# Moving the stack transfers of q to SyncE's queue and the loads of x one block later, in a fused attention and channel-mix kernel

## What is computed

```python
# attention: 16 heads of 16, in 4 groups that share k and v; token i sees tokens i-127 to i
q = (x @ Wq + bq); k = x @ Wk + bk; v = x @ Wv + bv
scores = einsum(q, k) / sqrt(16)
scores = where(mask, -1e9, scores)
out = softmax(scores) @ v
x = layernorm(x + (out @ Wo + bo))
# channel mix
xr = mu_r * x + (1 - mu_r) * x_prev
xk = mu_k * x + (1 - mu_k) * x_prev
x = layernorm(x + sigmoid(xr @ W_r.T) * (square(relu(xk @ W_k.T)) @ W_v.T))
```

## Time and profile before

| what | value |
|---|---|
| median of 3 runs | 511.7 us (510.95 to 513.18) |
| profiled execution | 514.49 us |
| its span, first to last instruction | 512.8 us |
| TensorE busy | 413.8 us, 81% |
| weight loads | 253.1 us, 49% |
| DVE busy | 340.2 us, 66% |
| ScalarE busy | 272.8 us, 53% |
| GpSimd busy | 290.0 us, 57% |
| DMA moved | 39.24 MB, 77 GB/s on average |
| mean granted TensorE clock | 0.902 |

### The profile page before, as it was taken

The page is one execution under the profiler, slowest core; times in us unless marked ns, Lnnn a source line. Parts: engine busy times, 40 slices in busy tenths (PEclk is TensorE's granted clock), DMA queues, the critical chain, the costliest instruction groups (busy, mean ns, idle before and its releaser), DMA issues.

```text
span 512.8 us, 8346 instructions
## 1 busy us (share of the span) xinstructions
PE 413.8 (81%) x2494; PEld 253.1 (49%) x2494; DVE 340.2 (66%) x851; ACT 272.8 (53%) x566; POOL 290.0 (57%) x466
## 2 busy tenths in 40 slices
PE   5407767998699959998699958998699949999963
PEld 2105344565356545565356545565355635666452
DVE  5315534588577848788497848688578838888543
ACT  3301334665447735775367735775467725787642
POOL 5500334565557736675477736675567737777721
PEclk9856567999889978999799999999899969999988
DMA  7770493035802384034902384045902390000000
GB/s 287 140 90 7 112 150 59 7 82 92 155 11 66 75 136 91 12 83 94 168 13 64 76 131 98 11 87 94 164 13 66 74 133 13 13 12 24 22 10 31
DMA packets 49356, 39.24 MB, mean 77 GB/s; under 512 B 32160, under 2 KB 40864, under 8 KB 49184
## 3 DMA queue, kind: packets, MB, share of 16 engines
q1 hardware_dynamic: 42256, 25.73, 21.7%
q10 hardware_dynamic: 7056, 12.98, 16.7%
HBM read 26.38 MB, written 12.06 MB: 75 GB/s over the span
## 4 chain that ended last, share of the span: by engine, by line
PE 45%; DVE 19%; DMA 19%; ACT 5%; issue 5%; SPq 4%; POOL 1%; ACTq 1%; DVEq 0%; POOLq 0%
DMA qs<-max_rows 11%; PE av_ps L963 8%; PE proj_ps L876 8%; PE score_ps L949 7%; DMA qs<-q_parts 6%; PE gen L1054 5%; DVE neg_max L688 5%; PE max_ps L932 4%; PE gen L1043 4%; SPq L321 3%; PE gen L997 3%; DVE mix L763 3%; DVE q_tiles L680 2%; DVE y L782 2%; PE gen L1032 2%
## 5 line engine op out<-in xcount | busy, mean ns | idle before, releaser
L386 POOL TENSOR_SCALAR_AFFINE_SELECT probs<-probs 128x512 f32<-128x512 f32 x252 | 167.5, 674 | 156.4 <-ACT probs L521 154.0
L521 ACT ACTIVATE probs<-score_ps 128x512 f32<-128x512 f32 x252 | 148.5, 598 | 139.8 <-PE score_ps L949 118.3
L949 PE MATMUL score_ps<-qs,ks 98*128 98x512 bf16 x252 | 102.4, 408 | 45.3 <-DMA qs<-max_rows 27.5
L688 DVE TENSOR_REDUCE neg_max<-max_ps 128x3 f32<-128x480 f32 x144 | 87.5, 632 | 24.7 <-PE max_ps L932 24.2
L949 PEld LDWEIGHTS score_ps<-qs,ks 98*128 98x128 bf16 x252 | 25.0, 100 | 108.2 <-ACT probs L521 57.5
L963 PE MATMUL av_ps<-probs,vals 128*32 128x512 f32 x504 | 70.5, 634 | 0.9 <-POOL probs L386 0.8
L932 PE MATMUL max_ps<-ks,q_tiles 96*128 96x160 bf16 x416 | 55.6, 254 | 0.0
L876 PE MATMUL proj_ps<-x_t,first 128*128 128x512 f32 x88 | 47.2, 663 | 9.3 <-DMA first<-w_first 5.5
L763 DVE SCALAR_TENSOR_TENSOR mix<-diff,first,x_t 128x128 f32<-128x128 f32 x128 | 50.7, 440 | 0.0
L393 POOL TENSOR_TENSOR rstd<-var,minus_half 128x1 f32<-128x1 f32 x64 | 35.7, 558 | 18.7 <-DVE var L712 17.7
L378 POOL TENSOR_TENSOR parts<-rest,parts 128x512 bf16<-128x512 f32 x24 | 30.3, 1266 | 27.7 <-ACT parts L503 27.7
(11 more groups left out here) (74 smaller groups left out, 631.4 us busy)
## 6 DMA issues: line engine op xcount, KB each, us to landing
qs<-q_parts ACTq DMA_DIRECT2D x48, 256.0 KB, 9.7
q_parts<-parts SPq DMA_DIRECT2D x48, 128.0 KB, 2.2
x_t<-x_feat SPq DMA_DIRECT2D x8, 512.0 KB, 11.9
x_in<-x_nat SPq DMA_DIRECT2D x8, 512.0 KB, 15.3
out<-out_t SPq DMA_DIRECT2D x32, 128.0 KB, 1.7
ks<-k_parts SPq DMA_DIRECT2D x42, 80.0 KB, 2.9
qs<-max_rows SPq DMA_DIRECT2D x128, 2.0 KB
k_parts<-parts SPq DMA_DIRECT2D x8, 192.0 KB, 2.8
```

Of the source, the lines that this page charges most:

```text
L386: nc.gpsimd.affine_select(out=v, in_=v, compare_op=ALU.is_ge if i % 2 else ALU.is_gt, fill=0.0, base=0, pattern=[[0, HPG], [sign, BLK]], c ...
L521: nc.scalar.activation(probs[:, buf, i], score_ps[i % 2][:, :], ACT.Exp, scale=SCALE).then_inc(s_exp, 1)
L688: nc.vector.tensor_reduce(neg_max[:, TPB * i:TPB * i + n], max_bank(t, j, i)[:, 0:n * TILE_KEYS].rearrange("p (n k) -> p n k", k=TILE_KEYS ...
L949: nc.tensor.matmul(score_ps[i % 2][:, :].rearrange("p (h q) -> p h q", q=BLK), ks[0:ROWS + MPARTS, par, g, k0:k0 + BLK], qs[0:ROWS + MPART ...
```

## The change

`stack_q` becomes a function of SyncE's program. In `start()` it is called behind `stack_k`; in `step` it is called at j == 1, directly behind `max_in`. `load_x` moves from j == 1 to j == 2, there too behind `max_in`. The waits of `stack_q` and the transfers themselves are the same.

```diff
@@ SyncE @@
+            def stack_q(s, par, rep):
+                if rep == 0:
+                    sp.wait_ge(s_spill_q, s * SPILLS + SPILLS)
+                    if later(s, 2):
+                        sp.wait_ge(s_score, scored(s * SB_BLKS - SB_BLKS - 1, NSCORE - 1))
+                sp.dma_start(qs[rep * DH:(rep + 1) * DH, par].rearrange("d j (m x) g t -> d (j m) (x g t)", m=QCH),
+                             q_dram[par, Q_PART[rep]].rearrange("j m (d y) t -> d (j m) (y t)", d=DH)
+                             ).then_inc(s_stack, 16)
...
                 for rep in range(NREP):
                     stack_k(0, 0, rep)
+                for rep in range(NREP):
+                    stack_q(0, 0, rep)
                 max_in(0, 0, 0)
...
                 if project and j == 0:
                     spill_q(s + 1, 1 - par, 0)
                     spill_q(s + 1, 1 - par, 1)
-                if coming and j == 1:
+                if project and j == 1:
+                    for rep in range(NREP):
+                        stack_q(s + 1, 1 - par, rep)
+                if coming and j == 2:
                     load_x(s + 2, par)
                 if behind(t, j, scores, 5):
                     store(t - 5, (j - 5) % 2)
@@ ScalarE @@
-            def stack_q(s, par, rep):
...
                 high_part(1, 0)
-                for rep in range(NREP):
-                    stack_q(0, 0, rep)
                 middle_part(1, 0)
...
                 if scores and t:
                     exps(t, 4, j % 2)
-                if project and j == 1:
-                    for rep in range(NREP):
-                        stack_q(s + 1, 1 - par, rep)
                 if scores:
                     exps(t, 5, j % 2)
```

## The result

The changed kernel takes 490.47 us (median of 4 runs, 488.44 to 493.15) against 511.44 us before: a ratio of 0.9587 with a 95% interval of 0.9525 to 0.965. The profiled execution took 492.25 us, with a span of 490.5 us and a mean granted clock of 0.903. The forecast was 492 us. Ratios, here and in the experiments, leave out the slower executions that some kernels show (those over 1.5% above the fastest of the same kernel), so they can differ a little from the ratio of two medians.

A forecast was written before the change was run, and what follows sets the result against it. Bound: row transfers slow beside q's stacks, once per superblock. Profiled 514.5 us, less 27 over the superblocks, plus 7.5 for the clock, is 495.0; the runs' median lies 2.8 lower, so 492 us, range 476 to 507.

The forecast's parts named there:

- first issue to last landing: q's six stacks in block 1: 14.9 us from first issue to last landing, with 16.8 us as upper bound.
- X to block 3: From block 1's first score product (X) to block 3's: 27.3 us instead of 31.33, in superblocks 1 to 6.
- clock in block 3: Block 3, seven times: 2.3 us at half clock, costing 1.1 us each, 7.5 us together; bounds none and 19 us.
- start: Program start: q's stacks go behind the six of k; cost taken as nothing, bounds -0.8 and +0.8 us.
- The rows: Block 1: rows ahead of q land about 1.1 us after their last issue, so block 2 starts 6.3 us earlier.
- Rival B: Block 1: q behind the rows holds them up as much as before; block 2 at X+17.2, 512 us; chance 0.07.
- rival D: Rows land late by part (q's 16.8 us, or low clock for 5.7 us): 500 to 507 us; 0.80 with main case.
- The wait for q: End of block 2: DVE's copy q_tiles waits 2.5 us or more for q's landing at X+23.9.
- Rival A: q alone moves much faster, block 2 never waits: block 3 at X+22.4, 8.9 us a superblock, 455 us; chance 0.06.
- ScalarE: Block 1: 4.07 us of issuing per superblock leave ScalarE, with its 3.58 us hole and TensorE's 2.65 us.
- x later: Loads of x issued about X+19 or a little later, landing in time for TensorE at X+31.8; cost nothing.
- Rival C: Block 3: x_t lands too late and stops TensorE 7 us, net 3 us in six superblocks: 530 us; chance 0.07.

The follow-up runs named there:

- the split runs: Changed kernel with some of q's six stacks issued ahead of block 1's rows, the rest behind: three ahead from superblock 1 on 484.39 us, two ahead 477.59 us.
- the half-size transfer: Changed kernel bringing only half of q's bytes from superblock 2 on: 480.56 us, ratio 0.9359 to the kernel before the change.
- the quarters: Changed kernel with GpSimd's addition x_bo made as four quarter instructions, one behind each of four masks in block 2: 492.81 us.
- the best version: Changed kernel with two stacks of q ahead of block 1's rows, four behind, and x_bo added in four quarters: 461.84 us, ratio 0.9085 to the kernel before.
- the split of three and three with the quarters: Changed kernel with three stacks of q ahead of block 1's rows, three behind, and x_bo in four quarters: 467.87 us, ratio 0.9106 to the kernel before.

## Why the prediction was right

Time, range and sign held, and so did the mechanism; the term for the clock did not. Step by step, for superblocks 1 to 6 of the profiled execution:

| step | predicted | measured |
|---|---|---|
| block 1 | 10.9 us | 10.94 to 10.97 |
| q's first issue | X+9.0 | X+8.97 to X+9.02 |
| first issue to last landing | 14.9 | 13.5 to 16.1, mean 14.7 |
| copy to block 3's first score product | 3.4 | 3.0 to 4.2, mean 3.8 |
| X to block 3 | 27.3 | (189.03-23.83)/6 = 27.5 |
| X to block 3, superblock 0 | 25.0 | 23.8 |
| all seven | 27 us less | 26.8 us less |
| clock in block 3 | 7.5 us more | see below |
| start | 0 | 0.7 us more |

*The rows.* Rows run ahead of q, and where their landing can be bounded, in the run with q behind them on the other queue, it is at their quiet speed. That run, the run with q ahead of them, and the split runs show that it is the order that does it. Rival B (q holds the rows up as much from behind) is out: the wait for the rows fell from 30.1 to 2.9 us. So is rival D (rows late by part), as no block 1 was longer than 10.97 us. The rule of the Trainium skill, page "DMA: Bandwidth & Descriptors", section "Issuing engines are not separate DMA queues", holds here as far as it goes: transfers on either queue met on the same engines (8.3 us for the rows beside q against 1.1). Read as "only issuing time can be saved" it misses the case: the issuing time was worth nothing that can be measured here, and the order 4%.

*The wait for q.* It came where it was put, 1.9 to 4.5 us, 6.1 in superblock 0. That it was the bound is shown by the half-size transfer and by the quarters that changed nothing in the changed kernel. Rival A had the price of its absence right in kind: the best version begins block 3 at X+22.6, against the X+22.4 of that rival. But it needs the split and the quarters.

*ScalarE.* The step "4.07 us of issuing per superblock leave ScalarE, and with them the 3.58 us hole and TensorE's 2.65" took superblock 2 for all: the six issues took 3.5 us and left a hole of 3.0 in the other five of superblocks 1 to 6. It was right in kind in block 1 and worth nothing in sum, which the prediction's sum had implicitly, since block 3 hangs on q alone.

*The clock.* This is the step whose place was wrong. I put 1.1 us a superblock, 7.5 us in all, into block 3. In block 3 there was next to nothing: 14.03, 14.24, 14.03, 14.11, 15.17 us in superblocks 1 to 5 against 14.03 or 14.04 before, 1.4 us more together, and 1.2 us less in superblock 0. The loss lay in block 2 instead. There TensorE waited 2.6 us for DVE's mix, behind the copy that x_bo had stretched, and the clock was low in superblocks 2 to 5 already before q_tiles began, from 10.1 to 10.6 us into block 2. The waits for mix before the change and after it:

```profile
PE gen L1043 <- DVE mix L763: 7.2, 6, 2.0
```

```profile
PE gen L1043 <- DVE mix L763: 15.5, 6, 2.6
```

This wait alone does not decide it: superblocks 1 and 6 had it too and kept their clock at 1.00 up to block 3, as in superblock 1:

```profile
110.68:136.76 26.08, 21.36 (x156) 13.71 (x154) 22.23 (x55) 15.23 (x32) 17.97 (x29) 1.00 0.68 112
```

What decides between the two is open. Where the clock was low, the last term was 4.2 us instead of the 3.0 of superblock 1. A low clock inside block 3, as predicted, did come in superblock 5 (0.92), where q landed latest, and in every superblock of the run with q behind the landed rows (0.87 to 0.98). And 3.5 us lay at the end of the program, which no step mentioned. The 26.8 us less 0.2 in the blocks 3, 3.5 at the end and 0.7 at the start leave 22.4 us, which is the difference of the spans but for rounding; the prediction had 27 less 7.5, 19.5. That the two sums agree within 3 us is partly luck.

*x later.* "X+19 or a little later" was X+21.7, since the rows ahead of it were held up by the stretched DVE copy; with the addition in quarters it was X+19.7. It made no difference, as x_t landed 3.7 us after its issue there (median of all eight 4.4), and TensorE did not wait for it. Rival C never came near. The trace of before had row after row of 11.9 and 15.3 us for x, all of them beside q; without q x takes a third of that.

Left open is why q's landing varies from 13.5 to 16.1 us from one superblock to the next with nothing else in the queue, and what puts the end of the program at the low clock in some profiles: from the last block's first score product to the end it took 37.5 to 42.8 us over the profiles of this study.

## What to carry over

When a small transfer that an engine waits for shares the DMA engines with a large one, look for the moment when the large one is asked for, not for the engine that asks: behind the small one in the same queue it costs nothing, beside it or ahead of it, it cost some 6 us here. Then ask when the large one must have landed, for that becomes the bound; if there is room on both sides of the small one, split it so that each part fits its gap. And follow a gain to the next limit with its own experiment: the quarters of x_bo were worth nothing in the changed kernel and 16 us in the split one.

## What the hardware showed that was not expected

**A GpSimd addition holds a DVE copy up for its whole length.** The 128x1024 addition x_bo (2.36 us, two inputs in SBUF) stretched a DVE copy of 128x16 from 0.17 us to between 2.12 and 2.29 in six of six superblocks of the changed kernel, and each time the copy ended 0.03 us after the addition. The kernel before had the addition too, but there it met one of the products mix in four of six superblocks (2.44 us instead of 0.34) and the step after this copy in two. In the split of three and three with the quarters, DVE instructions that read PSUM (reciprocal, maxima) kept their 0.24 and 0.65 us inside a quarter. The Trainium skill, page "SBUF — State Buffer", section "SBUF: two separate sides", describes the port pair that DVE and GpSimd share as an exclusive lock for the whole instruction; the trace agrees. GpSimd's addition in the timeline of the changed kernel, to be read beside the copy at 178.92 above:

```profile
178.81 2.36 POOL L388 TENSOR_TENSOR x_bo<-x_in,rest_w 128x1024 f32<-128x1024 f32 x1
```

**ScalarE issues more slowly while SyncE issues the rows.** The six issues of q took 4.07 us on ScalarE in superblock 2 of the kernel before and 3.5 in five other superblocks, as in superblock 6:

```profile
409.75 3.54 ACTq L512 DMA_DIRECT2D qs<-q_parts  x6
```

They took 2.75 us on SyncE behind the rows, and 2.73 us on ScalarE when it waited for the rows first. Six 1 KB issues in the old place took 3.62 us. So the price is in the coincidence, not in the size. It falls on one side only, as the four row issues took 2.60 us on SyncE with and without ScalarE's beside them; and two engines at once are not enough for it, as at the start of the kernel before ScalarE took 2.75 us while SyncE issued stacks of k from 18.61 to 21.44:

```profile
20.31 2.75 ACTq L512 DMA_DIRECT2D qs<-q_parts  x6
```

**Long low-clock spells at the end.** Before and after differ there by 3.5 us in work that the change does not touch, at clocks of 0.93 and 0.77. So two profiles can differ by 3 us for this alone. Whether it is also behind the 4.7 us between the fastest and the slowest run of the changed kernel is not shown, as only one of those runs was profiled.
